# Attention inside a two-layer transformer kernel on one core: rows of queries and keys laid out by dimension, the keys loaded from GpSimd's queue

## The chip, the core and the metric

The kernel runs on one core of a Trainium2 chip. Its engines are TensorE (PE), VectorE (DVE), ScalarE (ACT), GpSimd (POOL) and SyncE (SP), which here only issues transfers; PE's weight loads are listed apart as PEld. Matrix products land in PSUM, everything else works in SBUF, and between SBUF and the chip's memory (DRAM) the data moves by 16 DMA engines. The metric is the time of one execution on the device in microseconds (us).

## What is computed

Two attention layers sit between mixture-of-experts layers. The input is 4096 tokens (2 sequences of 2048) of width 256; both attentions have 16 heads of dimension 16. Cut to what matters here:

```python
def _L0_attn_ref(x, Wq, bq, Wk, bk, Wv, bv, Wo, bo):
    ...
    scores = jnp.einsum('bhqd,bhkd->bhqk', q, k) / math.sqrt(Dh)
    ...
    scores = scores + alibi[None]
    scores = jnp.where(causal[None, None], scores, -jnp.inf)
    weights = jax.nn.softmax(scores, axis=-1)
    y = jnp.einsum('bhqk,bhkd->bhqd', weights, v)
    ...
def _L1_attn_ref(x, Wq1, Wq2, Wk1, Wk2, Wv, Wc, lq1, lk1, lq2, lk2):
    ...
    a1 = jax.nn.softmax(att1, axis=-1)
    a2 = jax.nn.softmax(att2, axis=-1)
    ...
    att = a1 - lam_full[None, :, None, None] * a2
    y = jnp.einsum('bhqk,bkhd->bqhd', att, v)
    ...
x = x + 0.5 * _L0_ffn_ref(...)
x = x + _L0_attn_ref(...)
x = x + 0.5 * _L0_ffn_ref(...)
x = x + 0.5 * _L1_ffn_ref(...)
x = x + _L1_attn_ref(...)
x = x + 0.5 * _L1_ffn_ref(...)
```

## The kernel before

The kernel runs the layers as phases, one after the other. Names of buffers begin with the phase: `bp` and `ep` are the projections of the first and the second attention (`project_phase`), `ba` and `ea` the attentions themselves (`attention_phase`).

**Projection.** A query or key value is kept as three bf16 numbers ("levels") that add up to the float32 value. A unit of the projection is one 128 x 512 block of one matrix: PE multiplies (L1165, four matmuls), ACT scales the product into float32 (`t`, L1193), DVE casts it to the first level (L1220), subtracts (`res`, L1223), and casts the second level (L1225), GpSimd subtracts the third (L1243), and SyncE's queue stores all three in DRAM (`lv`, L1145). `t`, `res` and the PSUM block have two buffers, the levels four. `bp` has 32 such units, `ep` 64. Then follow 32 tiles of values (`vd`), and the phase ends.

**Attention.** A step handles four score matrices (four heads in `ba`, two heads with two maps each in `ea`): 8 steps in `ba`, 16 in `ea`. The operands `qx` and `kx` have two buffers, so the rows of step st+1 are loaded while step st is worked on. The product of two three-level numbers is taken over 96 partitions: query levels times key levels in six pairs (`LEVEL_PAIRS`). Partitions hold the first query level three times over against key levels 0 to 2, the second twice against 0 and 1, the third once against 0. To these come constant rows (12 for `ba`, which carry the position bias, 3 for `ea`), among them the three rows from partition MR on in which GpSimd stores the negated row maxima in levels, against ones on the key side.

Each head is loaded by itself on SyncE's queue (`load`, L1434 to L1439): for each group of two heads 12 transfers of 48, 32 or 16 rows of 4 KB and two of constants, 28 for a step (`nld` is the number per group). A third transfer kind, `vx` (L1444), brings the values. In a step (`body` of `sync`) that queue first takes the softmax sums of the step before through DRAM (`sums_out`), waits for that step's last value product (s_av), loads group 0 and the values, takes the inverses of the sums back and spreads them into `rec` (`inverses_in`, L1456 and L1461), loads group 1, and stores results (L1467, L1470).

PE's order in a step is written out by `step_order`: score blocks B (L1557) in query blocks Q = 0 to 3 of 512 columns, 40 units of four, with value products V (L1572) behind them; and between them, in shares, the products A of the maxima (L1532), which DVE reduces (L1670). The maxima of a step's own later tiles come in the first 19 units; from unit 19 on (`NEXT_AT`) come the first maxima of the next step, and before the first of them PE waits once for the next step's two groups of loads. In `ea` the difference of the two maps is a matmul on `rec` (C, L1579), first at unit 18.

GpSimd stores the maxima rows of a step in three kinds (`store_maxima`, L1504, four transfers each; kind 0 for tiles 0 to 7, kind 1 for 8 to 11, kind 2 for 12 to 15) and multiplies output and inverses (`scaled`, L1509). Score blocks with Q = 2 (units 12 on) wait for kind 1, those with Q = 3 for kind 2, and the step's first block for kind 0. PE's wait at the start of each attention is for both groups of step 0:

```python
                for g in range(2):
                    pe.wait_ge(s_ld[0][g], 16 * nld)
```

## Time and profile before

| | us |
|---|---|
| median of 3 runs | 6747.85 |
| lowest and highest of them | 6737.48, 6751.71 |
| profiled execution | 6750.49 |
| its span in the trace | 6748.4 |
| PE busy in the span | 5221.8 (77%) |
| DVE busy | 3307.6 (49%) |
| ACT busy | 2556.6 (38%) |
| GpSimd (POOL) busy | 1576.2 (23%) |

The span runs from the first to the last instruction; 2.1 us of the execution lie outside it. Busy shares are means over phases with different limits. Matmuls are pipelined and their ends are modelled, so PE at 77% is not PE at its peak. A row's bracket gives the idle time of the engine before the instruction and what ended it; where a wait is for several transfers, the profile names the one that came last.

### The profile page before, as it was taken

How to read it: one execution, taken by the hardware profiler on the slowest of the kernel's cores; microseconds unless marked ns; L12 is line 12 of the kernel's file. 1: busy time of each engine (PE TensorE's matmuls, PEld its weight loads, DVE VectorE, ACT ScalarE, POOL GpSimd, SP SyncE). 2: the span in 40 equal slices, each digit the busy share in tenths (PEclk: the TensorE clock that was granted, in tenths of full speed). 3: DMA queues.
4: the chain of work that ended last, by engine and by line, in shares of the span. 5: the costliest groups of instructions: out<-in, count | busy, mean ns of one | idle time of the engine just before them, and what ended most of it. 6: DMA issues, size and time to landing. Idle time of an engine off the chain costs nothing. (4 is left out here: it accounts for less than half of the span.)

```text
span 6748.4 us, 94042 instructions
## 1 busy us (share of the span) xinstructions
PE 5221.8 (77%) x30108; PEld 2792.5 (41%) x30112; DVE 3307.6 (49%) x4783; ACT 2556.6 (38%) x5006; POOL 1576.2 (23%) x1276
## 2 busy tenths in 40 slices
PE   6566558888787566489968688888888888977997
PEld 3454223333225355248943233333323333344686
DVE  7411646666545621311157566666666666543011
ACT  2311116655561311122221265556555665612221
POOL 2488200000001288333323000000000001002332
PEclk9678769999898687789989699999999999988998
DMA  2476431112103277408945111111111111011498
GB/s 93 114 149 131 144 95 42 42 48 62 56 27 111 74 153 148 115 0 295 315 162 161 47 34 45 52 38 34 46 51 37 34 47 50 16 62 35 160 314 274
DMA packets 454295, 660.14 MB, mean 98 GB/s; under 512 B 97984, under 2 KB 308992, under 8 KB 448672
## 3 DMA queue, kind: packets, MB, share of 16 engines
q1 hardware_dynamic: 383232, 544.50, 25.8%
q0 software_dynamic: 70656, 110.44, 8.1%
q8 instruction: 228, 3.74, 0.2%
q14 instruction: 179, 1.47, 0.1%
HBM read 489.33 MB, written 164.20 MB: 97 GB/s over the span
## 5 line engine op out<-in xcount | busy, mean ns | idle before, releaser
L1670 DVE TENSOR_REDUCE ea_mx<-ea_psA 128x1 f32<-128x1024 f32 (+7 forms) x1280 | 1317.0, 1061 | 691.8 <-PE ea_psA L1535 484.4
L1652 ACT ACTIVATE ea_pr<-ea_psB 128x512 f32<-128x512 f32 (+3 forms) x2560 | 1229.5, 535 | 928.6 <-PE ea_psB L1557 508.1
L1532 PE MATMUL ea_psA<-ea_kx,ea_qx 99*128 99x512 bf16 (+3 forms) x2560 | 728.5, 362 | 284.3 <-DMA ea_kx<-in_c_k 255.0
L1670 DVE TENSOR_REDUCE ba_mx<-ba_psA 128x1 f32<-128x1024 f32 (+7 forms) x640 | 657.2, 1061 | 379.3 <-PE ba_psA L1535 279.9
L1557 PE MATMUL ea_psB<-ea_qx,ea_kx 99*128 99x512 bf16 (+3 forms) x2560 | 782.2, 354 | 29.1 <-issue 21.1
L1652 ACT ACTIVATE ba_pr<-ba_psB 128x512 f32<-128x512 f32 (+3 forms) x1280 | 610.7, 535 | 493.3 <-PE ba_psB L1557 259.4
L1572 PE MATMUL ea_psO<-ea_pr,ea_vx 128*32 128x512 f32 (+3 forms) x5120 | 610.5, 549 | 1.9 <-ACT ea_pr L1652 0.4
L1532 PE MATMUL ba_psA<-ba_kx,ba_qx 108*128 108x512 bf16 (+3 forms) x1280 | 370.5, 368 | 197.9 <-DMA ba_kx<-in_c_k 180.1
L1532 PEld LDWEIGHTS ea_psA<-ea_kx,ea_qx 99*128 99x128 bf16 x2560 | 217.5, 100 | 691.9 <-issue 378.5
L1504 POOL DMA_DIRECT2D ea_qx<-ea_mT x192 | 105.6, 557 | 1540.0 <-DVE ea_mT L1692 1515.8
L1557 PEld LDWEIGHTS ea_psB<-ea_qx,ea_kx 99*128 99x128 bf16 x2560 | 242.3, 99 | 500.9 <-ACT ea_pr L1652 315.0
L1557 PE MATMUL ba_psB<-ba_qx,ba_kx 108*128 108x512 bf16 (+3 forms) x1280 | 387.0, 354 | 13.1 <-issue 6.7
L1572 PE MATMUL ba_psO<-ba_pr,ba_vx 128*32 128x512 f32 (+3 forms) x2560 | 305.3, 549 | 1.3 <-ACT ba_pr L1652 0.4
L1532 PEld LDWEIGHTS ba_psA<-ba_kx,ba_qx 108*128 108x128 bf16 x1280 | 109.0, 101 | 408.2 <-issue 230.5
L1504 POOL DMA_DIRECT2D ba_qx<-ba_mT x96 | 52.9, 558 | 800.5 <-DVE ba_mT L1692 800.2
L1535 PE MATMUL ea_psA<-all_cb 128*128 128x128 bf16 x1024 | 228.1, 234 | 0.0
L1557 PEld LDWEIGHTS ba_psB<-ba_qx,ba_kx 108*128 108x128 bf16 x1280 | 120.1, 99 | 232.0 <-ACT ba_pr L1652 154.8
L718 POOL DMA_INDIRECT acc<-ce_y,c_idx x128 | 205.0, 1601 | 45.5 <-issue 35.5
L718 POOL DMA_INDIRECT acc<-ae_y,a_idx x128 | 204.5, 1598 | 43.8 <-issue 36.5
L1560 PE MATMUL ea_psB<-all_cb 128*128 128x128 bf16 x1024 | 209.4, 222 | 0.0
L1509 POOL TENSOR_TENSOR ea_rec<-ea_osb,ea_rec 128x2048 f32<-128x2048 f32 x16 | 72.5, 4531 | 542.2 <-DMA ea_rec<-sums 542.2
L1059 DVE TENSOR_SCALAR fe_gs<-fe_g 128x256 f32<-128x256 f32 x64 | 24.0, 376 | 313.9 <-DMA fe_g<-rows,f_idx 313.9
(524 smaller groups left out, 8248.3 us busy)
## 6 DMA issues: line engine op xcount, KB each, us to landing
de_wg<-in_L_rg SPq DMA_DIRECT2D x64, 512.0 KB, 4.6
de_wu<-in_L_ru SPq DMA_DIRECT2D x64, 512.0 KB, 5.7
de_wd<-in_L_rd SPq DMA_DIRECT2D x64, 512.0 KB, 7.2
fe_wg<-in_L_rg SPq DMA_DIRECT2D x64, 512.0 KB, 4.6
fe_wu<-in_L_ru SPq DMA_DIRECT2D x64, 512.0 KB, 5.6
fe_wd<-in_L_rd SPq DMA_DIRECT2D x64, 512.0 KB, 7.0
ae_w<-in_L_w SPq DMA_DIRECT2D x64, 384.0 KB, 3.8
ce_w<-in_L_w SPq DMA_DIRECT2D x64, 384.0 KB, 3.5
```

The source lines that it names most:

```text
L718: nc.gpsimd.indirect_dma_start(out=acc[a], out_offset=column(n, a), in_=y[:, n % RING, a, :], in_offset=None, bounds_check=bound, oob_is_e ...
L1059: nc.vector.tensor_scalar(gs[:, u % 4, :], g[:, u, 0:H], g[:, u, H:H + 1], None, ALU.mult).then_inc(s_gs, 1)
L1504: pool.dma_start(qx[MR:MR + 3, s, hh, t0 * P:(t0 + tc) * P].rearrange("l (t q) -> l t q", q=P), mT[hh * 3 * tc:(hh + 1) * 3 * tc, k, :]).t ...
L1509: nc.gpsimd.tensor_tensor(rec[:, s, :], osb[:, s, :], rec[:, s, :], ALU.mult).then_inc(s_z, 1)
L1532: last = nc.tensor.matmul(psA[:, slot, at:at + n], qx[0:KB, s, hh, t * P:(t + 1) * P], kx[0:KB, s, hh, k:k + n], start=True, stop=not diag)
L1535: last = nc.tensor.matmul(psA[:, slot, at + n - P:at + n], C["identb"], C["maskA"], start=False, stop=True)
L1557: last = nc.tensor.matmul(psB[:, slot, off:BLK], kx[0:KB, s, hh, kt * P:(kt + 1) * P], qx[0:KB, s, hh, Q * BLK + off:(Q + 1) * BLK], start ...
L1560: last = nc.tensor.matmul(psB[:, slot, off:off + P], C["identb"], C["maskB"], start=False, stop=True)
L1572: last = nc.tensor.matmul(psO[hh * VW:(hh + 1) * VW, off:BLK], vx[:, s, kt, vcol:vcol + VW], pr[:, j % 2, hh, off:BLK], start=(kt == 0), s ...
L1652: nc.scalar.activation(pr[:, j % 2, hh, off:BLK], psB[:, exp_slot(n, s), off:BLK], ACT.Exp).then_inc(s_exp, 1)
L1670: v.tensor_reduce(out, src, AX.X, ALU.max).then_inc(s_ar, 1)
```

## The change

1. The projections lay out query and key rows by dimension and not by head: the host permutes the columns of the weights (`together`), so that the four heads of a step stand side by side for each dimension. In DRAM the rows of one dimension, for the four heads of a step, are then 16 KB in one piece. Queries and keys have one DRAM tensor each (`lvq`, `lvk`).
2. SyncE's queue loads the queries with one transfer for each repeat count (3, 2, 1) and, in `ba`, one of constants: 3 or 4 transfers and not 14 for the queries, all at the place where group 0 stood. Keys move to GpSimd's queue in as many (`load_keys`), in the order 32, 16, 48 rows, at the head of the step, behind a wait for s_av, ahead of the store of kind 1.
3. The constant rows move behind the 96 level rows; the maxima rows are last (MR = KA), the ones opposite them are loaded once per phase, and the maxima products leave these three rows out. The score products still have 108 and 99 rows; the maxima products have 105 and 96.
4. In the projection, ACT writes the first level itself, by a second activation from PSUM; DVE does subtract, cast, subtract; GpSimd does nothing.

```diff
@@ project_phase @@
-                    after(act, s_r, n, 2, first)
+                    after(act, s_lo, n, 2, first)
...
+                    nc.scalar.activation(t32[:, k % 2, :], ps[:, k % 2, :], f, scale=mats[m][2], **a)
+
+                    act.wait_ge(s_out[k % NL], ((b * QB + i) * (nu // NL) + k // NL) * 16)
+                    nc.scalar.activation(lev[:, k % NL, 0], ps[:, k % 2, :], f, scale=mats[m][2],
                                          **a).then_inc(s_t, 1)
...
-                    nc.vector.tensor_copy(lev[:, v, 0], t32[:, u, :]).then_inc(s_c, 1)
+                    nc.vector.tensor_tensor(res[:, u, :], t32[:, u, :], lev[:, v, 0], ALU.subtract).then_inc(s_c, 1)
                     dve.wait_ge(s_c, base + n * 2 + 1)
-                    after(dve, s_lo, n, 2, first)
-                    nc.vector.tensor_tensor(res[:, u, :], t32[:, u, :], lev[:, v, 0], ALU.subtract).then_inc(s_c, 1)
+                    nc.vector.tensor_copy(lev[:, v, 1], res[:, u, :]).then_inc(s_c, 1)
                     dve.wait_ge(s_c, base + n * 2 + 2)
-                    nc.vector.tensor_copy(lev[:, v, 1], res[:, u, :]).then_inc(s_r, 1)
+                    nc.vector.tensor_tensor(lev[:, v, 2], res[:, u, :], lev[:, v, 1], ALU.subtract).then_inc(s_lo, 1)
...
-            @block.gpsimd
-            def _(pool):
-                def rest(n, b, i, k, m, half, first):
...
@@ attention_phase, sync @@
+                def load_queries(st, s):
+                    at = 0
+                    for n in (3, 2, 1):
+                        src = lvq[3 - n, ds(st * HV * DH, HV * DH), :].rearrange("(d h) s -> d (h s)", h=HV)
+                        sp.dma_start(qx[at:at + n * DH, s].rearrange("p h s -> p (h s)"),
+                                     src.unsqueeze(0).broadcast_to((n, DH, HV * S))).then_inc(s_lq[s], 16)
+                        at += n * DH
+                    if F:
+                        sp.dma_start(qx[KP:KA, s].rearrange("p h s -> p (h s)"), qc[ds(st * F, F), :]).then_inc(s_lq[s], 16)
...
-                        load(st + 1, 1 - s, 0)
+                        load_queries(st + 1, 1 - s)
                     if prev:
                         inverses_in(st - 1, 1 - s, use + s - 1)
-                    if nxt:
-                        load(st + 1, 1 - s, 1)
...
@@ attention_phase, gpsimd @@
+                def load_keys(st, s):
+                    at = {3: 0, 2: 3 * DH, 1: 5 * DH}
+                    for n in (2, 1, 3):
+                        pool.dma_start(kx[at[n]:at[n] + n * DH, s].rearrange("p h s -> p (h s)"),
+                                       lvk[0:n, st * HV * DH:(st + 1) * HV * DH, :].rearrange("l (d h) s -> l d (h s)", h=HV)
+                                       ).then_inc(s_lk[s], 16)
...
                 def body(st, s, use, prev, nxt, before):
+                    if nxt:
+                        if prev:
+                            pool.wait_ge(s_av, st * NU)
+                        load_keys(st + 1, 1 - s)
                     store_maxima(st, s, 1)
...
@@ attention_phase, tensor @@
-                        last = nc.tensor.matmul(psA[:, slot, at:at + n], qx[0:KB, s, hh, t * P:(t + 1) * P],
-                                                kx[0:KB, s, hh, k:k + n], start=True, stop=not diag)
+                        last = nc.tensor.matmul(psA[:, slot, at:at + n], qx[0:KA, s, hh, t * P:(t + 1) * P],
+                                                kx[0:KA, s, hh, k:k + n], start=True, stop=not diag)
...
-                for g in range(2):
-                    pe.wait_ge(s_ld[0][g], 16 * nld)
+                pe.wait_ge(s_lq[0], 16 * nld)
+                pe.wait_ge(s_lk[0], 16 * (lk0 + nld))
+                pe.wait_ge(s_one, 32)
```

What stands on SyncE's queue in a step of `ba`, before: the first of the two groups of loads, from the fetch of the sums on (ISA rows hold waits or registers).

```order
L1450 DMA sums<-ba_osb 4x2048 [waits ba_oev]
L1452 DMA ba_sm<-sums 128x64 [waits ba_sd1]
L1477 REGISTER_ALU
L1434 ISA [waits ba_av]
L1434 DMA ba_qx<-lv 48x1x2048
L1436 DMA ba_kx<-lv 48x1x2048
L1434 ISA
L1434 DMA ba_qx<-lv 48x1x2048
L1436 DMA ba_kx<-lv 48x1x2048
```

The same place after, from the wait for s_av down to the first of the four transfers into `rec`:

```order
L1420 ISA [waits ba_av]
L1420 DMA ba_qx<-lvq 48x1x8192
L1420 ISA
L1420 DMA ba_qx<-lvq 32x1x8192
L1420 ISA
L1420 DMA ba_qx<-lvq 16x8192
L1424 ISA
L1424 DMA ba_qx<-in_c_q 9x8192
L1425 ISA
L1425 DMA ba_vx<-vd 128x2048
L1437 DMA sums<-ba_sm 128x64 [waits ba_rc]
L1442 DMA ba_rec<-sums 32x2048 [waits ba_rd1,ba_yo1]
```

The key loads are gone from this queue, the query loads are four times as long, and the second group behind the transfers into `rec` is gone too.

GpSimd in a step of `ba`, before: the store of kind 0 for this step, then kind 1, the product with the inverses, kind 2.

```order
L1504 DMA ba_qx<-ba_mT 3x8x128 [waits ba_mT]
L1504 DMA ba_qx<-ba_mT 3x8x128 x3
L1504 DMA ba_qx<-ba_mT 3x4x128 [waits ba_mT]
L1504 DMA ba_qx<-ba_mT 3x4x128 x3
L1509 TENSOR_TENSOR ba_rec<-ba_osb,ba_rec 128x2048 [waits ba_rec1]
L1504 DMA ba_qx<-ba_mT 3x4x128 [waits ba_mT]
```

And after:

```order
L1485 DMA ba_qx<-ba_mT 3x8x128 [waits ba_mT]
L1485 DMA ba_qx<-ba_mT 3x8x128 x3
L1491 DMA ba_kx<-lvk 32x1x8192 [waits ba_av]
L1491 DMA ba_kx<-lvk 16x8192
L1491 DMA ba_kx<-lvk 48x1x8192
L1495 DMA ba_kx<-in_c_k 9x8192
L1485 DMA ba_qx<-ba_mT 3x4x128 [waits ba_mT]
L1485 DMA ba_qx<-ba_mT 3x4x128 x3
L1500 TENSOR_TENSOR ba_rec<-ba_osb,ba_rec 128x2048 [waits ba_rec1]
```

The next step's keys, with a wait of their own, now stand ahead of the store of kind 1.

## Rows read from the trace of the kernel before

**Rows 1.** The page: length of the profiled execution, and the two costliest waits' groups.
```profile
span 6748.4 us, 94042 instructions
...
L1532 PE MATMUL ea_psA<-ea_kx,ea_qx 99*128 99x512 bf16 (+3 forms) x2560 | 728.5, 362 | 284.3 <-DMA ea_kx<-in_c_k 255.0
...
L1532 PE MATMUL ba_psA<-ba_kx,ba_qx 108*128 108x512 bf16 (+3 forms) x1280 | 370.5, 368 | 197.9 <-DMA ba_kx<-in_c_k 180.1
```

**Rows 2.** Timeline of PE (start, length, ..., [idle before <-releaser]): maxima after loads.
```profile
937.05 0.26 PE L1532 MATMUL ba_psA<-ba_kx,ba_qx 108*128 108x128 bf16 x1 [58.42 <-DMA ba_kx<-in_c_k]
...
1168.05 0.26 PE L1532 MATMUL ba_psA<-ba_kx,ba_qx 108*128 108x128 bf16 x1 [20.61 <-DMA ba_kx<-in_c_k]
...
3763.30 0.27 PE L1532 MATMUL ea_psA<-ea_kx,ea_qx 99*128 99x128 bf16 x1 [54.42 <-DMA ea_kx<-in_c_k]
...
3990.87 0.26 PE L1532 MATMUL ea_psA<-ea_kx,ea_qx 99*128 99x128 bf16 x1 [14.37 <-DMA ea_kx<-in_c_k]
```

**Rows 3.** Windows: length, busy PE, PEld, DVE, ACT, POOL, PEclk, DMA share, GB/s.
```profile
3931.00:3976.00 45.00, 44.06 (x304) 16.05 (x305) 35.35 (x36) 32.10 (x69) 6.70 (x5) 1.00 0.33 93
3976.00:3991.00 15.00, 0.64 (x4) 0.17 (x4) 1.11 (x6) 1.08 (x2) 0.00 (x0) 0.68 0.20 63
3991.00:4059.00 68.00, 66.36 (x454) 25.41 (x453) 49.05 (x56) 42.94 (x89) 4.44 (x8) 0.97 0.04 8
```

**Rows 4.** Timeline of SyncE's queue (SPq) in both attention phases.
```profile
883.25 0.94 SPq L1434 DMA_DIRECT2D ba_qx<-lv  x1
...
1103.42 0.83 SPq L1434 DMA_DIRECT2D ba_qx<-lv  x1
...
3713.43 0.90 SPq L1434 DMA_DIRECT2D ea_qx<-lv  x1
...
3931.38 0.82 SPq L1434 DMA_DIRECT2D ea_qx<-lv  x1
...
3959.95 1.73 SPq L1461 DMA_DIRECT2D ea_rec<-sums  x4
3961.77 0.77 SPq L1434 DMA_DIRECT2D ea_qx<-lv  x1
```

**Rows 5.** Timeline of GpSimd in one step.
```profile
3932.05 2.16 POOL L1504 DMA_DIRECT2D ea_qx<-ea_mT  x4 [31.71 <-DVE ea_mT L1692]
3967.06 4.54 POOL L1509 TENSOR_TENSOR ea_rec<-ea_osb,ea_rec 128x2048 f32<-128x2048 f32 x1 [32.84 <-DMA ea_rec<-sums]
```

**Rows 6.** Timeline of PE: query block 2 begins; first matmul of L1579.
```profile
1128.07 0.59 PE L1557 MATMUL ba_psB<-ba_qx,ba_kx 108*128 108x512 bf16 x2
...
3956.02 0.60 PE L1557 MATMUL ea_psB<-ea_qx,ea_kx 99*128 99x512 bf16 x2
...
3972.87 1.07 PE L1579 MATMUL ea_psA<-ea_rec,all_cf 128*64 128x512 f32 x2
```

**Rows 7.** DMA issues: a store of the maxima rows, KB each, us to landing.
```profile
ea_qx<-ea_mT POOLq DMA_DIRECT2D x128, 3.0 KB, 1.7
```

**Rows 8.** Instructions of the projection: ns min/median/max, first and last start.
```profile
L1225 DVE CAST ep_lev<-ep_res x64: 426/427/429, 3502.2 to 3652.5; 128x512 bf16<-128x512 f32 x64
L1225 DVE CAST bp_lev<-bp_res x32: 426/427/428, 756.4 to 831.5; 128x512 bf16<-128x512 f32 x32
...
L1223 DVE TENSOR_TENSOR ep_res<-ep_t,ep_lev x64: 691/1524/1528, 3501.5 to 3651.0; 128x512 f32<-128x512 f32 x64
...
L1193 ACT ACTIVATE bp_t<-bp_ps,bp_bias x32: 687/687/688, 754.5 to 827.3; 128x512 f32<-128x512 f32 x32
```

**Rows 9.** Timeline of the projection: DVE's first unit, and PE's four matmuls of one.
```profile
3501.51 0.69 DVE L1223 TENSOR_TENSOR ep_res<-ep_t,ep_lev 128x512 f32<-128x512 f32 x1
3502.24 0.43 DVE L1225 CAST ep_lev<-ep_res 128x512 bf16<-128x512 f32 x1
3502.70 0.43 DVE L1220 CAST ep_lev<-ep_t 128x512 bf16<-128x512 f32 x1
...
3644.28 1.98 PE L1165 MATMUL ep_ps<-ef_xnT,ep_w 128*128 x4 [0.37 <-ACT ep_t L1193]
```

More of the change, by code:

```diff
@@ L1109, in project_phase @@
         psV = sc.ps("psV", [P, 2, BLK])
-        s_w, s_vw, s_mm, s_t, s_c, s_r, s_lo, s_vm, s_vs, s_vi = (
-            sc.sem(n) for n in ("w", "vw", "mm", "t", "chain", "r", "lo", "vm", "vs", "vi"))
+        s_w, s_vw, s_mm, s_t, s_c, s_lo, s_vm, s_vs, s_vi = (
+            sc.sem(n) for n in ("w", "vw", "mm", "t", "chain", "lo", "vm", "vs", "vi"))
         s_out = [sc.sem(f"out{u}") for u in range(NL)]
@@ L1326, with attention_phase @@
 FIRST_MAXIMA = [e for i in range(CUT) for e in [("A", (0, i))] + [(k, (0, KIND_LAST.index(i))) for k in "LM" if i in KIND_LAST]]
-def attention_phase(nc, name, D, C, lvq, lvk, vd, yT, sums, sgn, maps, qc, kc, F, MR, s_m, st0):
+def attention_phase(nc, name, D, C, lvq, lvk, vd, yT, sums, sgn, maps, qc, kc, ones, F, s_m, st0, s_lk, lk0):
     two = maps == 2
     steps = B * NHEAD * maps // HV
-    KB = F + KP
-    shared = qc.shape[0] == F
+    KA, KB = KP + F, KP + F + 3
+    MR = KA
     VCOL = vd.shape[-1] // KT
     YR = P // maps
-    nld = 14
+    nld = 4 if F else 3
     SR = DH if maps == 1 else VW - 1
@@ L1352, in attention_phase @@
         psO = sc.ps("psO", [P, BLK])
-        s_ld = [[sc.sem(f"ld{s}{g}") for g in range(2)] for s in range(2)]
+        s_lq, s_one = [sc.sem(f"lq{s}") for s in range(2)], sc.sem("one")
         s_v = [sc.sem(f"v{s}") for s in range(2)]
@@ L1485, in body @@
                             result_out(st - 1, 1 - s, Q)
-                load(0, 0, 0, 1)
+                load_queries(0, 0)
+                for u in range(2):
+                    sp.dma_start(kx[KA:KB, u], ones.unsqueeze(1).broadcast_to((3, HV, S))).then_inc(s_one, 16)
                 steps_of(sp, body)
@@ L1517, in body @@
                         store_maxima(st + 1, 1 - s, 0)
+                load_keys(0, 0)
                 store_maxima(0, 0, 0)
@@ L1613, in body @@
                                 arrived = True
-                                for g in range(2):
-                                    pe.wait_ge(s_ld[1 - s][g], 16 * nld * (use + s + 1))
+                                pe.wait_ge(s_lq[1 - s], 16 * nld * (use + s + 1))
+                                pe.wait_ge(s_lk[1 - s], 16 * nld * (use + s + 1) + 16 * lk0)
                             maxima(i, 1 - s if d else s, slot)
@@ L1977, in constants @@
         "c_f16": row(p).astype(np.float16), "c_bf16": bf16(np.concatenate([h[n] for n, _ in BF16_CONSTS], 1)),
-        "c_q": bf16(q.reshape(-1, S)), "c_k": bf16(k.reshape(-1, S)),
-        "c_q1": bf16(np.zeros((3, S))), "c_k1": bf16(np.ones((3, S))),
+        "c_q": bf16(q.transpose(0, 2, 1, 3).reshape(-1, HV * S)),
+        "c_k": bf16(k.transpose(0, 2, 1, 3).reshape(-1, HV * S)), "c_one": bf16(np.ones((3, S))),
     }
@@ L2021, in macaron_kernel @@
     routed = scratch("routed", (T + P, H))
-    lv = [scratch(f"lv{i}", (3, B * H, S), BF16) for i in range(4)]
+    lvq, lvk = (scratch(n, (3, B * NHEAD * 2 * DH, S), BF16) for n in ("lvq", "lvk"))
     vd0, vd1 = scratch("vd0", (B * NHEAD // 4, P, KT * 4 * VW)), scratch("vd1", (B * NHEAD // 2, P, KT * 2 * VW))
@@ L2029, in macaron_kernel @@
         s_g0, s_s0, s_g1, s_o1 = lasting("gather0_", RING), lasting("scatter0_", S0), lasting("gather1_", RING), lasting("scatter1_", NY1)
-        s_m = lasting("maxima", len(KINDS))
+        s_m, s_lk = lasting("maxima", len(KINDS)), lasting("keys", 2)
         with Scope(nc, "in") as si:
@@ L2094, in lay_out @@
     D["L0_w"] = np.concatenate(up + [I["L0_ffn_w2"].transpose(0, 2, 1)], 2)
-    for n in "qkv":
-        D["L0_w" + n] = by_chunk(I["L0_attn_W" + n].T)
-    D["L0_bqk"] = np.concatenate([I["L0_attn_b" + n].reshape(HC, P).T for n in "qk"], 1)
+    together = lambda a, heads: a.reshape(-1, NHEAD // heads, heads, DH).transpose(0, 1, 3, 2).reshape(-1, H)
+    for n in "qk":
+        D["L0_w" + n] = by_chunk(together(I["L0_attn_W" + n].T, HV))
+    D["L0_wv"] = by_chunk(I["L0_attn_Wv"].T)
+    D["L0_bqk"] = np.concatenate([together(I["L0_attn_b" + n], HV).reshape(HC, P).T for n in "qk"], 1)
     D["L0_bv"] = I["L0_attn_bv"]
@@ L2107, in lay_out @@
         D["L1_" + k] = I["L1_ffn_" + n]
-    for n in ("q1", "q2", "k1", "k2", "v", "c"):
+    for n in ("q1", "q2", "k1", "k2"):
+        D["L1_w" + n] = by_chunk(together(I["L1_attn_W" + n], HV // 2))
+    for n in ("v", "c"):
         D["L1_w" + n] = by_chunk(I["L1_attn_W" + n])
```

49 lines of the change are left out of this document (13 added, 36 removed).

## The prediction, made before the changed kernel was run

> **What bounds the kernel now.** I read the page's costliest groups first, then the timeline of PE around their waits, then the windows of one step and the timelines of the two queues. The page shows one wait for a transfer that stands out in both attentions: before the maxima products PE stood idle until `kx` had come, 255.0 us in `ea` and 180.1 us in `ba` [rows 1]. The timeline parts each sum in two. The first wait of each phase is 54.42 and 58.42 us [rows 2]; the rest is 200.6 us over the 14 later steps of `ea` (14.3 each) and 121.7 us over 6 of `ba` (20.3 each). The shown waits of 14.37 and 20.61 us are the first of these.
>
> Is that wait on the path that sets the end? In the windows of a step PE is busy 44.06 of the 45 us ahead of it and 66.36 of the 68 behind it, and in the 15 us of the wait PE, DVE and ACT do together under 3 us of work [rows 3]. Nothing runs beside it, so what it loses the kernel loses. In those 15 us the DMA share is 0.20 at 63 GB/s: about 3 of 16 engines (0.20 x 16) carry all the load. Its length is thus set by how much lies on the few busiest engines, not by the chip's bandwidth. PE's granted clock is 0.68 of full in the wait and 0.97 in the 68 us behind it: the low level of 1.2 GHz lasts into the next work, and costs 68 x 0.03 = 2.0 us more a step.
>
> What do the loads take? At a phase's start queries and keys of four heads go out together, and PE starts 53.8 us after the first issue in `ba` (883.25 to 937.05) and 49.9 us in `ea` (3713.43 to 3763.30) [rows 2, 4]. In a step of `ea` group 0 starts at 3931.38; the transfers into `rec`, queued behind it, go at 3959.95; group 1 starts at 3961.77 and is there at 3990.87, 29.1 us later [rows 2, 4]. Half of a step's bytes takes some 25 to 29 us, wherever one looks.
>
> **The projection.** A unit takes (3652.5 - 3502.2) / 63 = 2.39 us in `ep` and (831.5 - 756.4) / 31 = 2.42 us in `bp` [rows 8]. DVE bounds it: its subtraction has a median of 1524 ns and a minimum of 691 [rows 8], and the short one is the first, with GpSimd not yet at work [rows 9]. With GpSimd's subtraction gone I price both of DVE's at 0.73 from start to start and the cast at 0.46 [rows 9]: 1.92 us. The second subtraction writes bf16, which no row shows without GpSimd; its bounds are a cast's 0.46 and the slow 1.52 + 0.04. At the upper end a unit takes 2.75 us and the 96 units lose 33 us; I take 0.73, since nothing is left that slowed the first. ACT does two activations of at most 0.69 [rows 8], 1.37 us, hidden behind either. PE's four matmuls are 1.98 us [rows 9], so PE is late next. Gain: 0.41 x 64 + 0.44 x 32 = **40 us** (45 with 1.92 us).
>
> **The start of each attention.** Queries keep SyncE's queue with half the bytes, and keys go at the same time from GpSimd's. If they don't hinder each other, 53.8 and 49.9 become 26.9 and 24.9: **52 us** gained; if they do, nothing. I take the first. The ones (3 rows) and the values ahead of them are small beside it. Later gains don't depend on this one.
>
> **The loads of each step.** Queries start at 3931.38 and are there by 3956.3 (24.9 on) to 3960.5 (29.1 on); PE asks for them at 3990.87 - 14.37 = 3976.5. In `ba` it is 1103.42 + 26.9 = 1130.3 against 1168.05 - 20.61 = 1147.4. Keys alone take no longer. At least 16 us are left, so the whole wait goes: 200.6 + 121.7 = **322 us**, and with it the low clock behind it, 20 x 2.0 = **40 us** (bounds 0 and 40; I take 40, as PE is never idle long enough in rows 3 for the clock to fall but in this wait). Late next is PE itself, at 98% busy.
>
> **What the moves put in the way.** (a) GpSimd issues four transfers of maxima rows in 2.16 us [rows 5]; three or four key transfers should cost as much, so the store of kind 1 issues 2.2 us later. It lands in 1.7 us [rows 7], and query block 2 begins 24.0 us after the store's old issue (3932.05 to 3956.02, rows 5 and 6): hidden. But its bytes can now queue behind the keys'. (b) The inverses in `ea` have little room: the product on GpSimd ends at 3967.06 + 4.54 = 3971.6 [rows 5] and PE needs it at 3972.87 [rows 6], 1.3 us later. They waited behind group 0, until 3959.95; now they wait behind the queries, as many bytes, and I leave them there at no cost. (c) Three rows fewer in the maxima products change no column count: nothing. (d) SyncE's queue issues fewer transfers; it was never waited for by itself.
>
> **The sum.** 40 + 52 + 322 + 40 = 454 us. The profiled execution's span is 6748.4, its time 6750.49, the median of the runs 6747.85: the span is within 1 us of the median and I count from it. 6748 - 454 = **6294 us**.
>
> The Trainium skill, DMA: Bandwidth & Descriptors, section Issuing engines are not separate DMA queues, speaks against this change: transfers started by SyncE and by GpSimd end on the same 16 engines and interleave, and a second issuing engine saves issue time alone. By that nothing of the 52 us would come, and the rivals A and C below would be the rule. The same page, section Why a DMA increments its semaphore by 16 and not by 1, says that a transfer runs on as many engines as divide its outermost dimensions (3 for 48 rows in three copies, 2 for 32), on SyncE's queue always the lowest ones, on GpSimd's consecutive ones that move on from transfer to transfer. By that keys and queries seldom meet, and the sum would stand. The share of 0.20 agrees with the count of engines; no row shows which engines they are.
>
> **Rival B: a part comes back as new waits.** The store of kind 1 stands behind the keys. If those take what half the bytes took, 24.9 to 29.1 us, it lands at 3931.4 + 24.9 + 1.7 = 3958.0 to 3962.2, and PE waits 2.0 to 6.2 us at block 2; in `ba` 1103.4 + 26.9 (29.1) + 1.7 = 1132.0 (1134.2) against 1128.07 [rows 6]: 3.9 to 6.1 us. Over 14 and 6 steps: 51 to 123 us, so 6345 to 6417. With some steps in which keys and queries meet and the inverses come 5 us late too, up to 6500. For it: the store's order is certain, the margin is 23 us. Against: it only has to wait for what is on its own engines.
>
> **Rival A: one set of engines for both queues.** Then queries and keys of a step take 49.9 us together in `ea`, to 3981.3. The inverses come behind the queries, and from the transfers into `rec` to the end of the product it takes 3971.6 - 3959.95 = 11.65 us: 3992.9 against 3972.87. PE waits 20.1 at L1579 where it waited 14.3: 81 us lost over 14 steps. `ba` has no such product; there the loads are in at 1157.2, PE waits 9.8 instead of 20.3, and 63 us come back. With the projection: 6748 - 40 - 63 + 81 = 6726 us.
>
> **Rival C, slower: the maxima rows behind all the loads.** As A, but the store of kind 1 lands only when the shared engines are clear: 3981.3 + 1.7 = 3983.0 in `ea`, 27.0 us after block 2 is due; 1157.2 + 1.7 = 1158.9 in `ba`, 30.8 us after. The old wait is then covered (14.3 and 20.3). Net 12.7 x 14 + 10.5 x 6 = 241 us lost, 40 gained: 6949 us. It decides at 23 us: keys that clear the store's engines within 23 us of s_av cost nothing, each us above it costs one a step. Against it: the 0.20 share leaves 13 engines free for a queue that uses others.
>
> **Rival D: the wait stays.** Keys of 16 KB rows could come so slowly by GpSimd's queue that PE waits as before and only the projection gains: 6708 us. No row shows a large transfer of this kind on that queue, so it can't be excluded.
>
> **How the numbers follow.** Forecast 53 in 100, at 6294 (own range 6250 to 6345: 45 and not 40 for the projection and up to 2 us a step of other idle time below it; no clock gain above). B 29 in 100, D 5, A 5, C 8. To hold 8 in 10 the range takes the forecast and B: 6250 to 6500. Two executions of this kernel can be told apart from about 0.2%, 13 us. Faster: 53 + 29 + 5 + 3 of A = 90; same 2 (A's 22 us could shrink under that); slower 8.
>
> **What the profile after would show.** Right: PE's wait for `kx` gone but for two of 25 to 27 us at the starts; PEclk at 1.0 from step start over unit 19; DVE subtractions at about 0.69 us; projection units 2.0 us apart. B: waits of a few us in the score products (L1557 of before) at query block 2, released by the maxima store. A: waits at the difference. C: both attentions longer, 27 us waits at block 2. The forecast is wrong if keys and queries share their engines, whatever the issuing queue.

## The result and the profile after

| | before | after |
|---|---|---|
| median of 4 runs each, side by side, us | 6744.48 | 6586.28 |
| profiled execution, us | 6750.49 | 6596.02 |
| its span, us | 6748.4 | 6594.1 |

The changed kernel takes 0.9769 of the time before (95% interval 0.9749 to 0.9788): 158 us less. The forecast was 454 us less, and its range (6250 to 6500) doesn't hold the time.

The page after, the span and the groups that answer to [rows 1]:

```profile
span 6594.1 us, 92722 instructions
...
L1528 PE MATMUL ea_psA<-ea_kx,ea_qx 96*128 96x512 bf16 (+3 forms) x2560 | 733.2, 364 | 210.2 <-DVE ea_mx L1667 159.6
...
L1528 PE MATMUL ba_psA<-ba_kx,ba_qx 105*128 105x512 bf16 (+3 forms) x1280 | 373.9, 371 | 134.1 <-DVE ba_mx L1667 73.5
```

PE's largest wait at the maxima products is no longer one for a transfer but one for DVE, which has not yet emptied the ring of PSUM blocks. The waits of PE and then of DVE after (us in total, times, longest):

```profile
PE ea_psA L1528 <- DVE ea_mx L1667: 159.6, 61, 13.2
PE ba_psA L1528 <- DVE ba_mx L1667: 73.5, 37, 11.5
PE ba_psA L1528 <- DMA ba_kx<-in_c_one: 58.3, 1, 58.3
PE ea_psA L1528 <- DMA ea_kx<-in_c_one: 47.0, 1, 47.0
PE ea_psA L1575 <- POOL ea_rec L1500: 25.7, 3, 18.1
...
DVE ea_sm L1694 <- DMA ea_sm<-sums: 186.9, 15, 40.9
DVE ba_sm L1694 <- DMA ba_sm<-sums: 118.5, 7, 51.8
```

And the same lines of before:

```profile
PE ea_psA L1532 <- DVE ea_mx L1670: 25.8, 47, 0.7
...
PE ba_psA L1532 <- DVE ba_mx L1670: 15.5, 32, 0.7
...
DVE ba_sm L1697 <- DMA ba_sm<-sums: 52.0, 1, 52.0
DVE ea_sm L1697 <- DMA ea_sm<-sums: 41.2, 1, 41.2
```

The waits for `kx` in the steps are gone; the two left are the starts. DVE waited for `sm` once in each attention before, for the last step's sums, when it had no other work left (harmless). After, it waits in each step that has loads under way, 14 of `ea` and 6 of `ba`: 145.7 us more in `ea` and 66.5 more in `ba`. Why is plain from one step of `ea`: SyncE's queue, GpSimd, DVE, PE (start, length; idle before and what ended it).

```profile
3823.09 0.57 SPq L1431 DMA_DIRECT2D sums<-ea_osb  x1
3831.89 0.35 SPq L1433 DMA_DIRECT2D ea_sm<-sums  x1
3832.56 2.27 SPq L1420 DMA_DIRECT2D ea_qx<-lvq  x3
3835.03 0.35 SPq L1425 DMA_DIRECT2D ea_vx<-vd  x1
3848.96 0.33 SPq L1437 DMA_DIRECT2D sums<-ea_sm  x1
...
3821.34 1.72 POOL L1491 DMA_DIRECT2D ea_kx<-lvk  x3 [26.42 <-PE ea_psO L1568]
3826.68 2.20 POOL L1485 DMA_DIRECT2D ea_qx<-ea_mT  x4 [3.61 <-DVE ea_mT L1689]
...
3847.98 0.55 DVE L1694 RECIPROCAL ea_sm<-ea_sm 128x64 f32<-128x64 f32 x1 [11.18 <-DMA ea_sm<-sums]
...
3850.12 1.04 PE L1528 MATMUL ea_psA<-ea_kx,ea_qx 96*128 96x512 bf16 x2 [10.32 <-DVE ea_mx L1667]
```

GpSimd waits only for the last value product and issues the keys at 3821.34. SyncE's first transfer of the sums waits for ACT's eviction too and goes at 3823.09, behind them. The second transfer can follow it 8.8 us later, where a step of before (the rows further down) shows 2.25, and DVE is released at 3847.98, 16.1 us after the second one's issue. DVE works in a fixed order: its reciprocal stands ahead of the reductions, so it stops for 11.18 us, the ring fills, and PE stops for 10.32. The same place in a step of before, SyncE's queue and then DVE:

```profile
3928.46 0.59 SPq L1450 DMA_DIRECT2D sums<-ea_osb  x1
3930.71 0.36 SPq L1452 DMA_DIRECT2D ea_sm<-sums  x1
...
3942.09 0.54 DVE L1697 RECIPROCAL ea_sm<-ea_sm 128x64 f32<-128x64 f32 x1
```

There the reciprocal came 13.63 us after the first transfer of the sums, in its turn and without a wait. That was the room these two transfers had; in the changed kernel they need 24.89 us (3823.09 to 3847.98).

Transfers' median us to landing, before and then after, say the same of all steps:

```profile
ea_sm<-sums SPq DMA_DIRECT2D x16, 32.0 KB, 1.9
...
ba_sm<-sums SPq DMA_DIRECT2D x8, 32.0 KB, 1.8
```

```profile
ea_kx<-lvk POOLq DMA_DIRECT2D x16, 768.0 KB, 25.8
...
ea_sm<-sums SPq DMA_DIRECT2D x16, 32.0 KB, 17.6
...
ba_sm<-sums SPq DMA_DIRECT2D x8, 32.0 KB, 16.6
```

The window of that step after, and the windows of both attentions from PE's first product on, before and then after (columns as in [rows 3]):

```profile
3823.00:3868.00 45.00, 33.65 (x238) 12.73 (x237) 26.05 (x31) 23.39 (x55) 2.27 (x5) 0.89 0.44 108
```

```profile
937.00:2014.00 1077.00, 905.36 (x6168) 338.99 (x6168) 685.25 (x784) 622.51 (x1312) 84.82 (x104) 0.90 0.17 47
3763.00:5910.00 2147.00, 1857.65 (x12456) 688.53 (x12456) 1412.55 (x1644) 1252.88 (x2624) 173.65 (x208) 0.93 0.14 40
```

```profile
918.00:1949.00 1031.00, 912.86 (x6168) 339.97 (x6168) 689.61 (x784) 622.90 (x1312) 100.97 (x132) 0.93 0.19 47
3658.70:5765.00 2106.30, 1873.08 (x12456) 688.85 (x12456) 1413.41 (x1644) 1254.34 (x2624) 200.07 (x252) 0.94 0.17 40
```

The stretches shrink by 46.0 and 40.7 us. The balance of PE closes: 208.0 (255.0 to 47.0) and 121.8 (180.1 to 58.3) us of waits for loads went, 329.8 in all, starts included. Back came 133.8 and 58.0 of waits for DVE at the maxima, 7.2 at the difference, 14.6 at the transposes of the levels (L1537), and 22.9 of busy time for the same 18624 matmuls, 912.86 + 1873.08 against 905.36 + 1857.65. Most of this last part is the clock: summed over both stretches in pieces of 5 us, busy time times what the granted clock lacks of full is 105.5 us before and 124.3 after, 18.8 more. Net 93.3; the stretches and the starts (7.5) give 94.2. The projections give 55 more, 149 of the 154.3 us between the two spans.

### The profile page after: what moved, and what is told of

It reads as the page before. It is cut to its first block and busy times, and to the rows that moved or that the text cites. A ratio compares the mean times of both kernels' runs of the same rounds, so it can differ in the third digit from the quotient of the medians.

```text
span 6594.1 us, 92722 instructions
## 1 busy us (share of the span) xinstructions
PE 5224.1 (79%) x30112; PEld 2796.2 (42%) x30112; DVE 3258.3 (49%) x4783; ACT 2607.7 (40%) x5102; POOL 1501.0 (23%) x1260
## 5 line engine op out<-in xcount | busy, mean ns | idle before, releaser
L1528 PE MATMUL ea_psA<-ea_kx,ea_qx 96*128 96x512 bf16 (+3 forms) x2560 | 733.2, 364 | 210.2 <-DVE ea_mx L1667 159.6
L1553 PE MATMUL ea_psB<-ea_qx,ea_kx 99*128 99x512 bf16 (+3 forms) x2560 | 789.7, 357 | 28.2 <-issue 20.3
L1528 PE MATMUL ba_psA<-ba_kx,ba_qx 105*128 105x512 bf16 (+3 forms) x1280 | 373.9, 371 | 134.1 <-DVE ba_mx L1667 73.5
L1528 PEld LDWEIGHTS ea_psA<-ea_kx,ea_qx 96*128 96x128 bf16 x2560 | 216.3, 100 | 615.5 <-DVE ea_mx L1667 336.6
L1528 PEld LDWEIGHTS ba_psA<-ba_kx,ba_qx 105*128 105x128 bf16 x1280 | 108.8, 100 | 343.8 <-DVE ba_mx L1667 179.8
L795 DVE TENSOR_TENSOR ce_h<-ce_sg,ce_psH 128x256 f32<-128x256 f32 x64 | 27.0, 421 | 302.5 <-ACT ce_sg L776 267.7
L795 DVE TENSOR_TENSOR ae_h<-ae_sg,ae_psH 128x256 f32<-128x256 f32 x64 | 27.0, 421 | 301.3 <-ACT ae_sg L776 250.4
```

The lines of the kernel that those rows point to most:

```text
L1528: last = nc.tensor.matmul(psA[:, slot, at:at + n], qx[0:KA, s, hh, t * P:(t + 1) * P], kx[0:KA, s, hh, k:k + n], start=True, stop=not diag)
L1553: last = nc.tensor.matmul(psB[:, slot, off:BLK], kx[0:KB, s, hh, kt * P:(kt + 1) * P], qx[0:KB, s, hh, Q * BLK + off:(Q + 1) * BLK], start ...
```

## The experiments

Times are medians; ratios are to the kernel before in runs on the same chip. Diffs are against the changed kernel where nothing else is said.

**The projection alone.** The kernel before, with `project_phase` of the changed one.

> The kernel before with the projection of the changed kernel alone (second activation on ScalarE, three operations on VectorE, none on GpSimd); the attention as before. From the two traces (last res of a projection minus its first t, 18.8 us less in bp and 36.7 in ep) the time should be 6744 - 55 = 6689 us. Had the projection gained only what I forecast, 40 us, it would be 6704; if the later values or stores gave it back, 6740.

Measured: 6684.3 us, ratio 0.9915 (0.9898 to 0.9931), 59 us less by the medians. The part is independent and larger than my 40.

**Keys behind the sums.**

```diff
                             pool.wait_ge(s_av, st * NU)
+                            pool.wait_ge(s_sm[1 - s], 16 * (use + s))
                         load_keys(st + 1, 1 - s)
```

> The changed kernel with one more wait: GpSimd starts a step's key transfers only when the softmax sums of the step before are back in SBUF. Theory 1: the keys' 16 KB packets, issued ahead of the two small transfers of the sums, hold those up, DVE stands at the reciprocal and PE behind DVE. Then DVE's wait for ea_sm and ba_sm (187 and 119 us) falls under 20 us each, PE's wait for DVE at the maxima falls from 160 and 74 us to the 26 and 15 us of before, the low clock behind it goes too, and the time is 6586 - 190 to 220 = 6365 to 6395 us. Theory 2: the sums are slow because of the large query rows on the same queue, whatever the keys do; then the waits stay and the time is within 25 us of 6586. Theory 3: the stall only moves on to the inverses, which stand behind the queries; then DVE's wait goes, PE waits at the difference in ea instead, and only ba gains, some 80 us: 6500 us.

Measured: 6720.87 us, ratio 0.9972 (0.9961 to 0.9984). The values of `sm` land in 1.7 us again and DVE waits for them only once, at each phase's end, as theory 1 expected. But the time is 135 us above the changed kernel and not 190 to 220 below it: the maxima rows now stand behind the keys. PE's waits in this kernel, and then GpSimd and PE in one step:

```profile
PE ea_psB L1554 <- DMA ea_qx<-ea_mT: 220.4, 14, 24.1
PE ba_psB L1554 <- DMA ba_qx<-ba_mT: 112.9, 6, 23.7
```

```profile
3868.38 1.72 POOL L1491 DMA_DIRECT2D ea_kx<-lvk  x3 [32.90 <-DMA ea_sm<-sums]
3870.09 2.19 POOL L1485 DMA_DIRECT2D ea_qx<-ea_mT  x4
...
3903.30 1.03 PE L1554 MATMUL ea_psB<-ea_qx,ea_kx 99*128 99x512 bf16 x2 [11.90 <-DMA ea_qx<-ea_mT]
```

The keys go 1.85 us after the queries (3866.53) and not 11 us ahead of them; the store, right behind them, lets PE go on 33.2 us after its issue. This is rival B's wait in its place (block 2), at 15.7 us a step in `ea` (220.4 / 14) and 18.8 in `ba`, where B had 2.0 to 6.2. Taking one victim out from behind the keys put another there.

**Keys behind both.** As above, and the store of kind 1 ahead of both waits.

```diff
                 def body(st, s, use, prev, nxt, before):
+                    store_maxima(st, s, 1)
...
+                            pool.wait_ge(s_sm[1 - s], 16 * (use + s))
                         load_keys(st + 1, 1 - s)
-                    store_maxima(st, s, 1)
```

> As e1 (keys only after the sums are back), and in addition behind the store of the maxima rows of kind 1 on GpSimd. e1 took away the wait for the sums and got one of 16 to 19 us a step at query block 2 for those rows, whose last packets stood behind the keys. Theory 1 extended (each small transfer must be ahead of the keys on its engines): both waits are gone. The inverses, which e1 brought in at +46 us of the step, stay behind queries and keys, so in ea PE waits some 7 us a step at the difference; ba waits for nothing. Against the kernel before with the projection alone (6684): 7 us at the starts, 14 x 7 in ea with 2 us of low clock each, 20.3 + 2 in 6 steps of ba: 6684 - 7 - 126 - 134 = 6415 us, and 6380 to 6450 as a range. Rival: the order is worth nothing, since keys that start 5 us later are missed at unit 19 instead; then waits for ea_kx of 10 us and more and 6550 us.

Measured: 6524.05 us, ratio 0.9675 (0.9659 to 0.9692), 62 us below the changed kernel, but above theory 1's 6380 to 6450; the rival's 6550 is nearer, though not for its reason: PE waits for keys only 8.8 us in all. The wait for the sums is gone, that for the maxima rows is 2.6 us, and PE waits for a third small transfer, the inverses' (waits, then us to landing):

```profile
PE ea_psA L1576 <- POOL ea_rec L1500: 162.5, 15, 19.2
```

```profile
sums<-ea_sm SPq DMA_DIRECT2D x16, 32.0 KB, 26.0
```

The transfer stands behind the queries and takes 26.0 us where it took 14.5 before and 16.1 in the changed kernel; queries and keys now run at one time. The wait comes to 10.3 us a step ((162.5 - 18.5) / 14, the one wait of before taken off), where I had expected 7.

**Keys on SyncE's queue.** The same long rows, issued behind queries and values.

```diff
                         load_queries(st + 1, 1 - s)
+                        load_keys(st + 1, 1 - s)
```

> The changed kernel with the keys, in the same 16 KB rows, on SyncE's queue behind the queries; GpSimd issues no key transfer. Theory 1 (keys ahead of the sums are the trouble): the sums are fetched ahead of all loads, so DVE's wait for them is under 20 us in each phase. On the busiest engine 34 packets each of queries and keys at 0.61 us make 42 us, so the inverses, queued behind them, come some 14 us late for the difference in ea (14 steps, 196 us lost) while ba gains 80 us: about 6560 us, with PE waits at the difference. The start waits grow or stay, 54 and 45 us. Theory 2 (large rows in themselves slow the small transfers): DVE's wait for the sums stays at 10 us or more a step, and the time is above 6586 us.

Measured: 6820.05 us, ratio 1.0116 (1.01 to 1.0133), slower than before. The pattern is theory 1's (no wait for `sm` but the one at each phase's end), the size is not: the inverses stand behind everything, `sums<-ea_sm` lands after 42.4 us, PE waits 359.0 us in 15 waits for `ea_rec`, and `ba`, which was to gain 80 us, still waits 81.3 us for its keys in the steps. So with these long rows the second queue is worth 234 us, largely because it takes the keys out from ahead of the inverses. The Trainium skill, DMA: Bandwidth & Descriptors, section Issuing engines are not separate DMA queues, says that a second issuing engine saves issue time alone; for this kernel as a whole the measurement decides against it, since a queue also sets what stands behind what. Whether the loads themselves go faster on two queues is not shown: the start of `ba` takes 53.7 us on two and 63.8 on one (865.56 to 929.38), but there SyncE spent 17.8 us issuing step 0's queries, values and keys (865.56 to 883.37), and in the changed kernel 2.9 on the first two (864.26 to 867.17).

**Both spread.** Queries and keys in six transfers of 16 rows each, one for each pair of levels.

```diff
-                    for n in (3, 2, 1):
-                        src = lvq[3 - n, ds(st * HV * DH, HV * DH), :].rearrange("(d h) s -> d (h s)", h=HV)
+                    for i, (l, _) in enumerate(LEVEL_PAIRS):
+                        src = lvq[l, ds(st * HV * DH, HV * DH), :].rearrange("(d h) s -> d (h s)", h=HV)
+                        sp.dma_start(qx[i * DH:(i + 1) * DH, s].rearrange("p h s -> p (h s)"), src).then_inc(s_lq[s], 16)
...
-                    for n in (2, 1, 3):
+                    for i, (_, l) in enumerate(LEVEL_PAIRS):
+                        pool.dma_start(kx[i * DH:(i + 1) * DH, s].rearrange("p h s -> p (h s)"),
+                                       lvk[l, st * HV * DH:(st + 1) * HV * DH, :].rearrange("(d h) s -> d (h s)", h=HV)
```

> The changed kernel with queries and keys each in six transfers of 16 rows, not in one of 48, one of 32 and one of 16; same bytes, same rows of 16 KB, same queues. Theory 1 with the count of engines: a transfer of 48 rows in three copies runs on 3 engines, of 32 on 2, and those few engines set the time of a load and hold the small packets behind it. Six transfers over 16 engines put 6 packets of queries and 6 of keys on each and not 34: the starts fall from 54 and 43 us to about 20 (57 us gained), the DVE wait for the sums from 12 to 17 us a step to under 5 (150 to 200 us gained): 6330 to 6380 us. Theory 4: the loads are bound by the memory and not by how many engines carry them; then starts and waits stay and the time is 6586 within 30 us, or more, since the packets now stand ahead of the sums on all engines.

Measured: 6367.85 us, ratio 0.9446 (0.9425 to 0.9467), 218 us below the changed kernel, inside theory 1's range. DVE's waits for the sums are under its 5 us a step (2.2 in `ea`, 4.7 in `ba`), but the starts gained 16.1 us and not 57. Its waits, and the window of the loads in a step of `ea` (share 1.04: all 16 engines):

```profile
PE ea_psA L1524 <- DVE ea_mx L1663: 45.0, 57, 2.8
...
PE ba_psA L1524 <- DVE ba_mx L1663: 34.8, 37, 4.7
...
DVE ba_sm L1690 <- DMA ba_sm<-sums: 79.8, 7, 51.8
DVE ea_sm L1690 <- DMA ea_sm<-sums: 71.4, 15, 41.2
```

```profile
3740.00:3760.00 20.00, 16.87 (x124) 6.05 (x117) 14.14 (x21) 12.25 (x29) 2.92 (x6) 1.00 1.04 122
```

The difference to the changed kernel closes: 114.6 and 38.7 us of waits for DVE, 16.1 at the starts, 7.1 at the difference, 6.4 at the transposes, 43.2 of PE's busy time (5224.1 to 5180.9): 226.1 us, against 224.7 between the spans. The Trainium skill, DMA: Bandwidth & Descriptors, section Rules for kernel authors, says that an outermost dimension smaller than 16 confines a transfer to as many engines; the shares, 0.20 in [rows 3] and 1.04 here, agree.

**Keys alone spread.** The second half of that diff only.

> The changed kernel, with the keys alone in six transfers of 16 rows each, on GpSimd's queue as before; the queries stay in three transfers, which a few DMA engines carry. In the changed kernel the values of sm land 17.6 us (ea) and 16.6 us (ba) after their issue, and VectorE waits for them 186.9 and 118.5 us; with both spread it waits 71.4 and 79.8 us. Theory 1: it is the keys' long queue on a few engines that the two small transfers of the sums stand behind, since keys are issued before them, and queries after; with the keys spread VectorE's waits come down to 70 to 110 us in ea and the kernel to 6400 to 6450 us, though the inverses still stand behind the queries. Theory 2: both share the blame, as the queries of few engines last 24 to 35 us and delay the inverses and the maxima's rows: GpSimd's rec comes late and TensorE waits for it 10 us a step, 6460 to 6540 us.

Measured: 6595.03 us, ratio 0.978 (0.9763 to 0.9797): nothing gained over the changed kernel. The waits only changed hands:

```profile
PE ea_psA L1575 <- POOL ea_rec L1500: 177.2, 15, 18.4
PE ba_psA L1528 <- DMA ba_kx<-in_c_one: 62.5, 1, 62.5
PE ea_psA L1528 <- DMA ea_kx<-in_c_one: 53.7, 1, 53.7
...
DVE ba_sm L1694 <- DMA ba_sm<-sums: 77.5, 7, 51.9
DVE ea_sm L1694 <- DMA ea_sm<-sums: 68.4, 15, 41.1
```

159.5 us of DVE's waits went (186.9 - 68.4 and 118.5 - 77.5); 151.5 came at the difference and 10.9 at the starts. `sums<-ea_sm` lands after 28.2 us, behind the queries' long rows. In PE's waits, 158.7 us for DVE at the maxima went (159.6 - 40.9 and 73.5 - 33.5). Both expectations were too low. With both halves spread the waits go, with the keys alone they don't; the queries alone spread were not run.

**Spread, keys behind both.** The last order of the keys, with both spread.

> e5 (all loads in transfers of 16 rows over 16 engines) with the order of e7. Theory 1: e5 still has 2.2 us (ea) and 4.6 us (ba) a step of DVE's wait for the sums, which goes: 14 x 2.2 + 6 x 4.6 = 58 us less, 6368 - 58 = 6310 us, 6300 to 6340 as a range. Rival: those waits are replaced by later inverses (e5 had them 4 us ahead of the difference) and the time stays at 6368 within 13 us.

Measured: 6368.49 us, ratio 0.9442 (0.9423 to 0.9461), the same as with the spread alone, as the rival had it. DVE's waits in the steps are gone but the inverses are late (54.8 us at `ea_rec`, 18.6 with the spread alone): the order is worth nothing once the loads are short.

**Keys in 4 KB rows.** Each of the three key transfers cut by heads into four, the partitions as they were.

```diff
+                        for hh in range(HV):
+                            pool.dma_start(kx[at[n]:at[n] + n * DH, s, hh, :],
+                                           lvk[0:n, st * HV * DH:(st + 1) * HV * DH, :].rearrange("l (d h) s -> l h d s", h=HV)[:, hh]
```

> The changed kernel with the keys in 12 transfers of 4 KB rows, one for each head, on GpSimd's queue in the same place; queries stay at 16 KB. Theory 1, in the form that a small packet on an engine waits for one packet of the keys at a time: 8 packets of the sums' fetch on an engine wait for 8 of 4 KB (0.16 to 0.6 us each) and not 8 of 16 KB (0.6 to 2.5 us): the fetch falls from 17 us to about 5, DVE's wait to under 5 us a step, and the time is 6586 - 150 = 6440 us. Rival (what counts is how many bytes stand ahead on those engines, whatever their packets): the fetch stays at 15 us or more and the time at 6586, or worse by the nine further issues on GpSimd.

Measured: 6706.36 us, ratio 0.9947 (0.9929 to 0.9966), 120 us above the changed kernel. The sums did come sooner. DVE's waits for them:

```profile
DVE ea_sm L1696 <- DMA ea_sm<-sums: 100.5, 12, 40.9
DVE ba_sm L1696 <- DMA ba_sm<-sums: 77.8, 7, 52.0
```

Without the one at the end that is 4.3 us a step in both ((100.5 - 40.9) / 14 and (77.8 - 52.0) / 6), under theory 1's 5, from 10.4 and 11.1. The second transfer lands 14.3 us after issue (17.6 in the changed kernel), far from theory 1's 5. So the form of the keys' transfers is a part of the sums' delay, though rows of 4 KB don't remove it. But the time went up: PE waits 110.6 us for `ea_rec`, 55.3 and 27.3 for the maxima rows, and 84.3 and 75.0 at the starts (58.3 and 47.0 in the changed kernel), so the keys themselves take longer. The run changes the length of a row and the number of transfers together and doesn't part them.

**The start, queries first.** GpSimd's first keys wait until step 0's queries are in.

```diff
+                pool.wait_ge(s_lq[0], 16 * nld)
                 load_keys(0, 0)
```

> The changed kernel, with GpSimd's first key transfers of each attention held until the queries of step 0 have landed. It shows what each costs alone. If queries alone take half of what both took before (my 27 and 25 us) and the keys 21 (as step 1's keys took alone in the changed kernel), PE starts 48 and 46 us after the first issue, no later than now (53.7 and 42.5): then the two hindered each other fully when they ran together. If the queries alone take 40 us or more, it is the queries and what stands between them (values, ones) that set the start, and the keys had been hidden.

Measured: 6649.77 us, in one execution. With no keys beside them the queries took 38.0 us in `ba` (865.89 to 903.93), not the 26.9 of my sum, and the keys 41.0 more (to 944.88), not 21; together they need 53.7. So the two loads overlap, though each is slower than I took it for. The queries were not quite alone: the values and step 1's queries were issued right behind them.

**The start, step 1's loads held back.**

```diff
                             sp.wait_ge(s_av, st * NU)
+                        else:
+                            sp.wait_ge(s_lk[0], 16 * (lk0 + nld))
                         load_queries(st + 1, 1 - s)
```

> The changed kernel, with one wait added at each attention's start: SyncE issues the queries and values of step 1 only when step 0's keys have landed. In the changed kernel the first multiplication of ba runs 53.7 us after the first query issue (864.3 to 917.9), the one of ea 42.5 us (3616.2 to 3658.7). Theory 1: these starts are stretched by step 1's queries and values, which run on other DMA engines at the same time; with them held back, ba starts after 35 to 45 us and ea after 30 to 38, and nothing in the steps changes: 6560 to 6578 us. Theory 2: the start is set by step 0's own long rows on two or three engines and by the GpSimd keys beside them; both starts stay within 3 us, and the kernel within 0.1% of 6586. A start later than before would speak against both, and for step 1's loads coming late.

Measured: 6573.36 us, ratio 0.9742 (0.9724 to 0.9761). The starts fall to 47.8 (866.68 to 914.48) and 38.2 us (3604.02 to 3642.20) from 53.7 and 42.5: 10 us together. The time is in theory 1's range; the starts fell by more than theory 2's 3 us, but not as far as theory 1's 45 and 38.

**The start, spread.** The same wait in the spread kernel. (Its expectation names 1 MB of values for two steps; `ba` loads 1 MB of them in each step, `ea` 512 KB.)

> The kernel with queries and keys in six transfers of 16 rows each (6367.9 us), with the same wait: step 1's queries and values only when step 0's keys have landed. There the first multiplications came 44.3 us (865.4 to 909.7) and 35.7 us after the first query issue, with all 16 DMA engines busy (share 1.03) at 127 GB/s. Theory 1: the starts are bound by bytes, and of the bytes that run then, step 1's queries (768 KB) and the values (1 MB for two steps) are a good half; the starts fall to 25 to 30 us in ba and to 20 to 25 in ea, and the time to 6340 to 6355 us. Theory 2: the starts are set by how GpSimd's six transfers share the engines with SyncE's own six; they stay near 40 and 33, and the time at 6360 to 6370.

Measured: 6376.03 us, ratio 0.9451 (0.9434 to 0.9467). Starts 41.4 and 34.1 us, from 44.3 and 35.7: theory 2, with a time that can't be told from the plain spread's.

**The start, ones first.**

```diff
+                for u in range(2):
+                    sp.dma_start(kx[KA:KB, u], ones.unsqueeze(1).broadcast_to((3, HV, S))).then_inc(s_one, 16)
                 load_queries(0, 0)
-                for u in range(2):
-                    sp.dma_start(kx[KA:KB, u], ones.unsqueeze(1).broadcast_to((3, HV, S))).then_inc(s_one, 16)
```

> The changed kernel, with SyncE's two transfers of the three rows of ones (kx<-in_c_one, three descriptors of 16 KB each) issued ahead of step 0's queries and values, and not behind them. In the changed kernel, in the one that holds step 1's loads back, and in all others, the first multiplication of each attention is released by these rows, as the last that lands. Theory 1: they are late since they stand behind the queries' long rows and the values (1 MB a step in ba, 512 KB in ea) on their engines; ahead of them the start is released by the keys or the queries, 38 to 45 us after the first issue in ba (53.7 in the changed kernel) and 30 to 37 in ea (42.5): 6565 to 6577 us. Theory 2: the queries and keys land only just before them; both starts stay within 3 us, and the kernel within 0.1% of 6586.

Measured: 6583.65 us, ratio 0.9762 (0.9743 to 0.9781). The starts are 52.7 and 44.1 us; the releasers are `ba_qx<-in_c_q` and `ea_qx<-lvq`. Theory 2: the ones were last only by a little.

**The start, spread, all else held back.** In the spread kernel, ones first, and step 0's values as well as step 1's loads behind a wait for step 0's keys.

> The kernel with queries and keys in six transfers of 16 rows each (6367.9 us), with the rows of ones issued ahead of step 0's queries, and step 0's values and all of step 1's loads issued only when step 0's keys have landed. When only step 1's loads were held back there, the starts hardly moved (907.0 minus 865.6, 41.4 us in ba, from 44.3): keys landed 35.8 us after the first issue, and the ones 5.6 us behind them. Theory 1: values (1 MB in ba, sharing all 16 engines with the 1.7 MB of queries, keys and constant rows) and the ones behind them are what is left; the starts fall to 22 to 30 us in ba and 20 to 27 in ea: 6330 to 6350 us. Theory 2: queries and keys of 16-row transfers, 1.5 MB with all 16 engines at some 127 GB/s less, take their time alone: the starts stay within 3 us of 41 and 35, and the kernel at 6360 to 6375.

Measured: 6360.07 us, ratio 0.9433 (0.9415 to 0.9452), the lowest median of the study, though its interval overlaps that of the plain spread. Starts 36.3 us in `ba`, between the theories, and 32.6 in `ea`, within theory 2's 3 us, as the time is in its range. With nothing but queries, keys and constant rows under way, the window of `ba`'s start reads:

```profile
866.00:900.00 34.00, 0.00 (x0) 0.00 (x0) 0.00 (x0) 0.73 (x1) 3.56 (x7) 0.50 0.88 104
```

## Why the prediction was wrong, point by point

- **What bounds the kernel, and that the loads' wait would go:** right. It was idle time of all engines, and it is 0 in the steps after. My margin of 16 us for the loads held.
- **The projection, 40 us:** right in kind, short in size: 55 us. DVE's subtraction fell to a median of 684 ns from 1524, the second to 693 [rows 8]. I held PE's 1.98 us for the next bound; the units come 1.79 us apart, which is DVE's own three instructions back to back, and PE kept up.

```profile
L1221 DVE TENSOR_TENSOR ep_res<-ep_t,ep_lev x64: 682/684/693, 3442.9 to 3555.7; 128x512 f32<-128x512 f32 x64
...
L1225 DVE TENSOR_TENSOR ep_lev<-ep_res,ep_lev x64: 691/693/693, 3444.1 to 3556.8; 128x512 bf16<-128x512 f32 x64
```

- **The starts, 52 us:** wrong; 0.1 in `ba` and 7.4 in `ea`. I halved the old time with the bytes. With no keys beside them the queries took 38.0 us, and with the keys 53.7, so half the bytes on a queue didn't take half the time; the form of the transfers had changed too (16 KB rows in few transfers). Step 1's loads, issued at once behind, cost 10 of it; the order of the ones nothing that shows. Even with 16-row transfers, undisturbed, the start takes 36.3 and 32.6 us.
- **The step that failed most: the steps' waits and their clock, 322 + 40 us, of which 87 came.** It failed in "What the moves put in the way", (b). I priced only the inverses behind the queries, at nothing. I did not see that the two small transfers of the sums, on SyncE's queue, must now run beside the keys, which GpSimd issues ahead of them. That cost 191.8 us of PE's waits for DVE and 14.6 at the transposes. The order views printed ahead of the prediction showed it: the keys' wait is for s_av alone, the sums' for the eviction behind it. I had priced the keys as starting with the queries, at 3931.4, when both transfers of the softmax sums are already issued; in the changed kernel the keys set out 1.75 us ahead of the first one (3821.34 and 3823.09). That the sums are the cause is shown by holding the keys behind them: DVE's waits in the steps went.
- **The clock, 40 us:** wrong in sign for the work. It is 0.89 in the 45 us of the step shown, since the wait moved and didn't go. The means of the two stretches rose (0.90 to 0.93 and 0.93 to 0.94), as less of them is idle, but PE's busy time for the same matmuls grew by 22.9 us. I had written that PE is never idle long enough but in the wait removed, and so gave the new waits no clock (in that step the granted clock is 0.73 from 3838 to 3851 us and 0.82 in the 9 us after).
- **The store of kind 1, (a):** right for this kernel, no wait at block 2, but in part by luck: the keys went 11 us ahead of the queries, which no sum of mine had. With the keys 13 us later against the queries (behind the sums) the wait came, 15.7 and 18.8 us a step.
- **Rivals.** B had the right kind, a new wait behind the keys, with 29 in 100, but at the wrong victim and with 2 to 6 us a step where 9.6 came (191.8 / 20). A and C (one set of engines) didn't come in the changed kernel: keys and queries overlap. A's kind of wait, at the difference, did come when keys and queries were issued together (10.3 us a step with the keys behind both). D didn't come. The range ended at 6500 because B was priced for a victim with 23 us of room; the sums, which cross DRAM twice in a row, had 13.6.

What stays open: how the two queues' long transfers share the engines from packet to packet. The runs show which waits come and go, no row shows the engines. That the inverses' transfer ahead of the queries would gain more was not tried.

## What to carry to other kernels

Before moving a large load to another queue, list every small transfer under way at that time, with its slack, on any queue: a load in transfers of few rows can delay any of them, and removing one victim brings up the next (sums, maxima rows, inverses: 6586, 6721, 6524 us). Cut the load so that each transfer covers 16 rows before giving thought to order: done for queries and keys it was worth 218 us here, and the order then nothing; for the keys alone it was worth nothing. An engine that works in fixed order passes such a wait on, so read what stands behind the waiting instruction, too.

## What the runs showed of the hardware

- A 32 KB transfer that lands in 1.9 us with no large load ahead of it took 17.6 us when the keys, in 16 KB rows, had been issued ahead of it from another engine's queue, 14.3 with the keys in 4 KB rows and 4.2 with them in transfers of 16 rows; the inverses', as small, took 42.4 us behind both loads on its own queue.
- Six transfers of 16 rows of 16 KB keep all 16 engines busy (share 1.04) at only 122 GB/s. In an expert layer of the changed kernel a share of 0.95 moves 321 GB/s, and its long rows in a step of `ba` 135 at 0.73:

```profile
1082.00:1100.00 18.00, 16.16 (x120) 5.62 (x117) 11.41 (x17) 12.39 (x29) 2.98 (x6) 1.00 0.73 135
...
3150.00:3280.00 130.00, 126.30 (x949) 118.53 (x948) 22.65 (x45) 28.80 (x68) 47.69 (x46) 1.00 0.95 321
```

  So the busy share is no measure of rate: on 16 rows it rose and the rate didn't. The cause wasn't tested.
- The time of a load did not scale with its bytes: at the start of `ba` queries with no keys beside them took 38.0 us, queries and keys on two queues 53.7, both on SyncE's queue 63.8.
